# First layer: the softmax division moved behind the value products, and contexts split into high and low parts on GpSimd

## The reference

```
# layer 0: grouped attention, 32 query heads on 8 key/value heads, head size 16
q = x @ Wq + bq;  k = ctx @ Wk + bk;  v = ctx @ Wv + bv
attn = softmax(q k^T / 4 + mask);  out = (attn @ v) @ Wo + bo
x = layernorm(out + x) * gamma + beta
# layers 1 and 2: layernorm, cross attention with 16 heads of 128 and one learnt
# extra key and value (bias_k, bias_v), added to x
# last: x + gelu(layernorm(x) @ w_fc1 + b_fc1) @ w_fc2 + b_fc2
```

## Time and profile before

| | |
|---|---|
| median of three runs | 2411.67 us |
| profiled execution, its time | 2410.44 us |
| its span on the core | 2408.3 us |
| PE busy in the span | 97% |
| layer 0 loop of a half, t0(1) to t0(28) | 107.0 us (half 0), 107.6 us (half 1) |

### The profile page before, as it was taken

How to read it: one execution, slowest core, us unless ns; L and a number is a source line. 1 busy time by engine, 2 the same in 40 slices (tenths; PEclk the granted TensorE clock), 3 DMA queues, 4 the chain that set the end, 5 groups by cost and what they waited for, 6 DMA issues and landing times.

```text
span 2408.3 us, 35904 instructions
## 1 busy us (share of the span) xinstructions
PE 2336.5 (97%) x13616; PEld 1959.0 (81%) x13616; DVE 1210.4 (50%) x2037; ACT 870.4 (36%) x2511; POOL 813.9 (34%) x599
## 2 busy tenths in 40 slices
...
DMA packets 37797, 120.54 MB, mean 50 GB/s; under 512 B 3616, under 2 KB 3872, under 8 KB 37664
## 3 DMA queue, kind: packets, MB, share of 16 engines
...
## 4 chain that ended last, share of the span: by engine, by line
PE 85%; POOL 7%; ACT 3%; DVE 3%; issue 2%; DMA 0%; SPq 0%; POOLq 0%; ACTq 0%; DVEq 0%
PE PS L643 72%; PE PS L871 5%; PE PS L887 5%; PE PS L879 2%; POOL XN L471 1%; POOL HF L471 1%; POOL X L505 1%; ACT AT L1252 1%; POOL W L495 1%; POOL XN L464 1%; POOL P0D L471 1%; ACT PS L1252 1%; POOL W L420 1%; PE PS L743 0%; POOL P0D L464 0%
## 5 line engine op out<-in xcount | busy, mean ns | idle before, releaser
L643 PE MATMUL PS<-AT,W 128*128 128x512 f32 x2496 | 602.8, 391 | 8.7 <-DVE AT L1549 7.8
L643 PEld LDWEIGHTS PS<-AT,W 128*128 128x128 f32 x2496 | 465.3, 188 | 114.0 <-DVE AT L1549 14.8
L1428 DVE TENSOR_TENSOR X<-PS,X 128x512 f32<-128x512 f32 x416 | 286.1, 690 | 360.6 <-PE PS L643 353.5
L542 POOL TENSOR_TENSOR PR<-PR,RC 128x512 f32<-128x512 f32 x128 | 133.4, 1042 | 951.0 <-DVE RC L1636 951.0
L643 PE MATMUL PS<-W,CX 128*128 128x512 f32 x1632 | 403.8, 398 | 7.7 <-DVE Q L1453 4.1
L643 PE MATMUL PS<-CT,W 128*128 128x512 f32 x1584 | 394.2, 398 | 11.0 <-DVE CT L1423 11.0
L643 PE MATMUL PS<-WV,CT 128*128 128x512 f32 (+1 forms) x1920 | 367.1, 349 | 0.0
L643 PEld LDWEIGHTS PS<-W,CX 128*128 128x128 f32 x1632 | 298.0, 188 | 73.4 <-issue 8.3
L643 PEld LDWEIGHTS PS<-WV,CT 128*128 128x128 f32 x1920 | 308.7, 189 | 45.5 <-issue 0.8
L643 PEld LDWEIGHTS PS<-CT,W 128*128 128x128 f32 x1584 | 289.6, 189 | 65.7 <-issue 11.2
L1279 ACT ACTIVATE CX<-PS,VEC 128x512 fp32r<-128x512 f32 x128 | 88.3, 690 | 648.1 <-PE PS L887 648.1
...
## 6 DMA issues: line engine op xcount, KB each, us to landing
...
```

Of the source, the lines that this page charges most:

```text
L542: nc.gpsimd.tensor_tensor(PR[:, :, 0:P], PR[:, :, 0:P], RC[:, 0, 0:BT].unsqueeze(2).to_broadcast([P, BT, P]), ALU.mult).then_inc(norm_done, 1)
L643: ins = nc.tensor.matmul(out, lhs(c, a), rhs(c, b), start=(k == 0), stop=(k == total - 1))
L1428: V_.tensor_tensor(X[:, tile, :], PS[:, bank, :], X[:, tile, :], ALU.add).then_inc(done, 1)
```

## The change

The product with the reciprocals (`norm`) goes. PE transposes the probabilities as they come from the exponentials, and the context of a unit is multiplied with the reciprocals instead, once in four steps. For that the reciprocals of a step are widened from 8 to 128 columns (`widen`, POOL), transposed by PE (`rt0`) into score columns 256 to 511 of banks BS and BS+1, which were spare, and read from there by DVE (`cxnorm0`). ACT evicts the raw context (`cxraw0`); POOL makes its high and low parts (`context`). Three heads are first added in halves on POOL (`half_sums`), and DVE sums 192 columns where it summed 384. `bv` is added with the values. DVE adds a row tile (`row0`) between the mask's add and the maximum, and `rec0(s)` comes in step s behind them, where `rec0(s + 1)` stood ahead. The tables `SPLIT_AT` and `BO_AT` are spread anew (24 pieces and 8 tiles as before; two pieces each in steps 22 and 23), and at the end keys and values of layer 1 change places and banks. The diff, with its indentation reduced and cut to its core:

```diff
-BO_AT = {8: 0, 9: 1, 10: 2, 11: 3, 16: 4, 17: 5, 18: 6, 19: 7}
+BO_AT = {8: 0, 9: 1, 10: 2, 11: 3, 12: 4, 14: 5, 16: 6, 19: 7}
...
+CXF = in_arena("CXF", [P, 3, 2, BTOK], F32, 36864)
...
+HS = BVR[:, 1024:1024 + (KV0 - OWN) * P].rearrange("p (s h t) -> p s h t", s=2, t=P // 2)
+RC0 = BVR[:, 1536:2048].rearrange("p (s n) -> p s n", n=P)
...
-BANKS_FIRST, BANKS_TURN = (BPV, BB, BS, BS + 1), (BA, BB, BS, BS + 1)
-LAST_ROWS = (BS, BS + 1, BA, BPT)
+BANKS_FIRST, BANKS_TURN = (BS, BS + 1, BB, BPT), (BA, BB, BS, BS + 1)
+LAST_ROWS = (BA, BPT, BPV, BC)
...
-    def norm(s):
+    def half_sums(s):
+        pool.wait_ge(exp0, hf * STEPS0 + (s + 1))
+        if s >= 2:
+            pool.wait_ge(rc0, hf * STEPS0 + (s - 1))
+        z = P0[s % BUFS0].rearrange("p (h t) -> p h t", t=P)[:, OWN:KV0, :]
+        nc.gpsimd.tensor_tensor(HS[:, s % 2, :, :], z[:, :, 0:P // 2], z[:, :, P // 2:P], ALU.add).then_inc(half0, 1)
+    def widen(s):
         pool.wait_ge(rc0, hf * STEPS0 + (s + 1))
-        z = P0[s % BUFS0].rearrange("p (h t) -> p h t", t=P)
-        nc.gpsimd.tensor_tensor(z, z, RC[:, s % 2, :].unsqueeze(2).to_broadcast([P, KV0, P]),
-                                ALU.mult).then_inc(norm0, 1)
+        if s >= 4:
+            pool.wait_ge(rt_ps, hf * STEPS0 + (s - 3))
+        copy_hi(RC0[:, s % 4, :].rearrange("p (h d) -> p h d", d=HD0),
+                RC[:, s % 4, :].unsqueeze(2).to_broadcast([P, KV0, HD0])).then_inc(wide0, 1)
+    def context(u):
+        pool.wait_ge(cx0_n, hf * UNITS0 + (u + 1))
+        copy_hi(CX0[:, u % 3, 0, :], CXF[:, u % 3, 1, :]).then_inc(cx0_hi, 1)
+        pool.wait_ge(cx0_hi, hf * UNITS0 + (u + 1))
+        nc.gpsimd.tensor_tensor(CX0[:, u % 3, 1, :], CXF[:, u % 3, 1, :], CX0[:, u % 3, 0, :].bitcast(F32),
+                                ALU.subtract).then_inc(cx0_lo, 1)
...
-    norm(0)
     sub(2)
+    half_sums(0)
     for s in range(STEPS0):
-        if s + 1 < STEPS0:
-            norm(s + 1)
         if s == STEPS0 - 2:
             first_rows()
         if s + 3 < STEPS0:
             sub(s + 3)
+        if s + 1 < STEPS0:
+            half_sums(s + 1)
+        widen(s)
+        if s % 4 == 0 and s:
+            context(s // 4 - 1)
         if s in BO_AT:
             add_bo_tile(BO_AT[s])
...
+    context(UNITS0 - 1)
...
     def t0(s):
-        pe.wait_ge(norm0, s0 + (s + 1))
+        pe.wait_ge(exp0, s0 + (s + 1))
...
-            pe.wait_ge(cx0_lo, u0 + u)
+            pe.wait_ge(cx0_raw, u0 - hf + u)
...
+    def rt0(s):
+        pe.wait_ge(wide0, s0 + (s + 1))
+        pe.wait_ge(z0, s0 + min(s + 5, STEPS0))
+        if s % 4 == 0 and s:
+            pe.wait_ge(cx0_n, u0 + s // 4)
+        nc.tensor.transpose(PS[:, BS + s % 4 // 2, 256 + s % 2 * P:256 + (s % 2 + 1) * P], RC0[:, s % 4, :],
+                            IDENT[:]).then_inc(rt_ps, 1)
...
         if s == 0:
             k0(1)
         else:
+            rt0(s - 1)
             pv0(s - 1)
         if s + 4 < STEPS0:
             s0_(s + 4)
...
         if s == STEPS0 - 4:
             pe.wait_ge(z0, s0 + STEPS0)
-            keys(n1, 0, 0, w1, BS)
+            values(n1, 0, w1, None, (0, 1))
         if s == STEPS0 - 3:
-            values(n1, 0, w1, None, (0, 1))
+            values(n1, 0, w1, None, (2, 3))
         if s == STEPS0 - 2:
-            values(n1, 0, w1, None, (2, 3))
+            pe.wait_ge(xadd, x0 + 3 * BT)
+            keys(n1, 0, 0, w1, BA)
+    rt0(STEPS0 - 1)
     pe.wait_ge(w_ready[3], nq + G0)
+    pe.wait_ge(cx0_lo, u0 + UNITS0 - 1)
     pe.wait_ge(k_ev, n1 * 2 + 1)
     last_rows0(0, 0)
+    pv0(STEPS0 - 1)
     last_rows0(1, 0)
-    pv0(STEPS0 - 1)
     last_rows0(2, 0)
+    pe.wait_ge(v_ev, n1 * 2 + 1)
     last_rows0(3, 0)
     pe.wait_ge(cx0_lo, u0 + UNITS0)
...
         def first_unit():
-            norm_t(norm_index(hf, ly), 0, BANKS_FIRST, range(1))
+            norm_t(norm_index(hf, ly), 0, BANKS_FIRST, range(2))
             pe.wait_ge(k_ev, b0 * 2 + 2)
-            norm_t(norm_index(hf, ly), 0, BANKS_FIRST, range(1, 2))
-            for c in range(2, C):
-                pe.wait_ge(xadd, x_count(hf, b0) - BT + c - 1)
-                norm_t(norm_index(hf, ly), 0, BANKS_FIRST, (c,))
-            pe.wait_ge(v_ev, b0 * 2 + 1)
+            norm_t(norm_index(hf, ly), 0, BANKS_FIRST, range(2, 3))
+            pe.wait_ge(xadd, x_count(hf, b0) - BT + 2)
+            norm_t(norm_index(hf, ly), 0, BANKS_FIRST, range(3, C))
+            pe.wait_ge(v_ev, b0 * 2 + 2)
+            pe.wait_ge(xadd, x_count(hf, b0))
             values(b0 + 1, 1, lv, None, (0, 1))
-            pe.wait_ge(v_ev, b0 * 2 + 2)
             values(b0 + 1, 1, lv, None, (2,))
-            pe.wait_ge(xadd, x_count(hf, b0))
             queries(b0, 0, 0, lq, at_now)
...
-        nc.scalar.activation(VT[:, tb, :], PS[:, BB, :], ACT.Copy).then_inc(vt_ev, 1)
+        nc.scalar.activation(VT[:, tb, :], PS[:, BB, :], ACT.Identity, bias=VEC[:, COL_BV0:COL_BV0 + 1]).then_inc(vt_ev, 1)
...
-    def cxhi0(u):
+    def cxraw0(u):
...
-        nc.scalar.activation(CX0[:, u % 3, 0, :], PS[:, BB, :], ACT.Identity,
-                             bias=VEC[:, COL_BV0:COL_BV0 + 1]).then_inc(cx0_hi, 1)
+        nc.scalar.activation(CXF[:, u % 3, 1, :], PS[:, BB, :], ACT.Copy).then_inc(cx0_raw, 1)
...
+    def rtev0(u):
+        act.wait_ge(rt_ps, s0 + (u * 4 + 4))
+        act.wait_ge(o0_ps, hf * ROWS0 + (u - 1) // 2 * 4)
+        nc.scalar.activation(CXF[:, u % 3, 0, :].rearrange("p (a n) -> p a n", a=2), PS[:, BS:BS + 2, 256:512],
+                             ACT.Copy).then_inc(rt_ev, 1)
...
         if s % 4 == 0 and s:
-            cxhi0(s // 4 - 1)
+            cxraw0(s // 4 - 1)
         if s + 3 < STEPS0:
             e0(s + 3)
         if s == STEPS0 - 4:
-            first_keys(0, BS)
             warm(ACT.Sqrt)
-    cxhi0(UNITS0 - 1)
+        if s == STEPS0 - 2:
+            first_keys(0, BA)
+    rtev0(UNITS0 - 1)
...
+    def soft0(s, row=None):
...
+        if row is not None:
+            row0(row)
...
         dve.wait_ge(exp0, s0 + (s + 1))
-        V_.tensor_reduce(SUM0[:, s % 2, OWN:KV0], P0[s % BUFS0].rearrange("p (h t) -> p h t", t=P)[:, OWN:KV0, :],
-                         AXX, ALU.add).then_inc(sum0, 1)
-        if s >= 2:
-            dve.wait_ge(norm0, s0 + (s - 1))
+        dve.wait_ge(half0, s0 + (s + 1))
+        V_.tensor_reduce(SUM0[:, s % 4, OWN:KV0], HS[:, s % 2, :, :], AXX, ALU.add).then_inc(sum0, 1)
+        if s >= 4:
+            dve.wait_ge(wide0, s0 + (s - 3))
         dve.wait_ge(sum0, s0 + (s + 1))
-        V_.reciprocal(RC[:, s % 2, :], SUM0[:, s % 2, :]).then_inc(rc0, 1)
-    def cxlo0(u):
-        dve.wait_ge(cx0_hi, u0 + (u + 1))
-        V_.scalar_tensor_tensor(CX0[:, u % 3, 1, :], PS[:, BB, :], VEC[:, COL_BV0:COL_BV0 + 1],
-                                CX0[:, u % 3, 0, :].bitcast(F32), ALU.add, ALU.subtract).then_inc(cx0_lo, 1)
+        V_.reciprocal(RC[:, s % 4, :], SUM0[:, s % 4, :]).then_inc(rc0, 1)
+    def cxnorm0(u):
+        cx = CXF[:, u % 3, 1, :].rearrange("p (a n) -> p a n", a=2)
+        if u == UNITS0 - 1:
+            dve.wait_ge(pv0_ps, s0 + STEPS0)
+            dve.wait_ge(rt_ev, hf + 1)
+            ins = V_.tensor_tensor(CXF[:, u % 3, 1, :], PS[:, BB, :], CXF[:, u % 3, 0, :], ALU.mult)
+        else:
+            dve.wait_ge(cx0_raw, u0 - hf + (u + 1))
+            dve.wait_ge(rt_ps, s0 + (4 * u + 4))
+            if u < UNITS0 - 2:
+                dve.wait_ge(s0_ps, s0 + (4 * u + 9))
+            ins = V_.tensor_tensor(cx, PS[:, BS:BS + 2, 256:512], cx, ALU.mult)
+        ins.then_inc(cx0_n, 1)
...
     for s in range(STEPS0):
-        if s + 1 < STEPS0:
-            rec0(s + 1)
-        if s % 4 == 1 and s > 1:
-            cxlo0(s // 4 - 1)
         if s - 2 in Q_AT:
             qlo0(Q_AT[s - 2])
+        row = s - 1 if s - 1 in ROWS_AT else None
         if s + 3 < STEPS0:
-            soft0(s + 3)
+            soft0(s + 3, row)
+        elif row is not None:
+            row0(row)
         if s == 0:
             klo0(1)
-        if s - 1 in ROWS_AT:
-            n, t = ROWS_AT[s - 1]
-            if n < 2:
-                dve.wait_ge(bo_tile, hf * SEQ + (n * BT + t + 1))
-            add0(n, t, BA)
+        rec0(s)
+        if s % 4 == 0 and s:
+            cxnorm0(s // 4 - 1)
...
-    cxlo0(UNITS0 - 1)
+    cxnorm0(UNITS0 - 1)
```

More of the change, by code:

```diff
@@ L47 @@
 SPLIT_AT = {0: (3, (0,)), 1: (3, (1,)), 2: (3, (2,)), 3: (3, (3,)), 4: (0, (0,)), 5: (0, (1,)), 6: (0, (2,)), 7: (0, (3,)),
-            12: (2, (0,)), 13: (2, (1,)), 14: (2, (2,)), 15: (2, (3,)), 20: (1, (0, 1)), 21: (1, (2, 3)),
-            22: (3, (0,)), 23: (3, (1,)), 24: (3, (2, 3)), 25: (0, (0,)), 26: (0, (1,)), 27: (0, (2,)), 28: (0, (3,))}
+            11: (2, (0,)), 13: (2, (1,)), 15: (2, (2,)), 16: (2, (3,)), 17: (1, (0,)), 18: (1, (1,)), 20: (1, (2,)), 21: (1, (3,)),
+            22: (3, (0, 1)), 23: (3, (2, 3)), 25: (0, (0,)), 26: (0, (1,)), 27: (0, (2,)), 28: (0, (3,))}
 PIECES = sum(len(parts) for _, parts in SPLIT_AT.values())
```

(15 more changed lines are left out.)

8 lines of the change are left out of this document (5 added, 3 removed).

## The result

The changed kernel takes 2418.25 us, median of ten runs (2417.62 to 2419.97), where the kernel before takes 2411.65, also of ten (2409.78 to 2413.64): the ratio is 1.0030, with a 95% interval of 1.0022 to 1.0038. It is 6.6 us slower; I had said 8.3 us faster.

A forecast was written before the change was run, and what follows sets the result against it. PE, busy 97% of the span, was taken to bound the kernel, leaving gains only in layer 0's loops: 4.45 us in half 0 and 3.85 in half 1, together 8.3, from 2411.67 to 2403.4 us; range 2395 to 2411.

The forecast's parts named there:

- Half 0: 4.45. Half 1: 3.85. Together 8.3: Gains in us summed over layer 0's loops and their end: 2.0 + 0.85 + 1.0 + 0.6 and 1.4 + 0.85 + 1.0 + 0.6.
- the three rivals: All of PE's waits go, 2396.1 us (chance 0.12); no change, 2410.8 us (0.19); slower, 2427 us (0.07).
- signs of being wrong: Layer 0: `rt0` waits with out0; PE waits for ACT over 2 us per half, t0(8)-t0(22); DVE waits for half sums.
- the rival that I called slower: In full steps of layer 0, PE also waits for the reciprocals' transpose; at 0.5 us each, 2427 us; chance 0.07.
- The other two signs: PE waiting for ACT's evictions over 2 us per half between t0(8) and t0(22); DVE waiting for the half sums.
- Steps 1 to 7: Start of layer 0's loops: ACT sets the pace instead of POOL; 2.0 us gained in half 0, 1.4 in half 1.
- Steps 8 to 21: Middle of layer 0's loops: PE's work 54.3 us plus 1.5, 55.9 in all; 0.85 us gained per half.
- the light pair: Steps 14 and 15 of layer 0: ACT and late reciprocals make them 5.9 us against PE's 4.4, 1.5 more.
- Steps 22 to 27: Late in layer 0's loops: POOL's chain of widenings, pieces and context puts t0(28) at 23.0 us; 1.0 gained per half.
- The end: From t0(28) on: DVE's chain gains 1.1 us, the last context through POOL loses 0.5; net 0.6 gained per half.
- POOL's costs: Layer 0, per step: half sums 0.60 us, widened reciprocals 0.35; a context 1.9 us once in four steps.

The follow-up runs named there:

- e2: The changed kernel with SUM0 allocated behind the arena, so that the arena begins where it did in the kernel before; 2406.84 us, ratio 0.9983.
- e1: The kernel before with RC and SUM0 at the changed kernel's size, so that the arena begins 128 bytes later; 2423.64 us, ratio 1.0053.
- e9: e2 with DVE's row tile behind the maximum, as in the kernel before, not between mask add and maximum; 2404.97 us, ratio 0.9971.
- e8: e2 with DVE's product of a context behind the next mask add, where e2 has it ahead; 2410.46 us.
- e10: e2 without POOL's half sums, DVE summing all 384 columns itself; 2405.6 us, ratio 0.9976.

## Why the prediction was wrong

**The step that failed.** "Half 0: 4.45. Half 1: 3.85. Together 8.3": the sum has terms for layer 0 alone and takes every matmul behind it at its old length. The two enlarged tables were costed at nothing, without a word on what they move. That missing term measured 11.7 us (5.9 and 5.8 in e2's layers against the changed kernel's), larger than the whole forecast and of the other sign; e1 and e2 show it from both sides. None of the three rivals had it.

My signs of being wrong looked at the loops alone. One came up: `rt0` waits in a step with out0, step 25, 1.5 us for POOL's widening in each half, in the changed kernel and in e2 alike (below, half 0 of e2). It is that one of the 12 such steps, so the rival that I called slower did not come about as a loss in all full steps. I had put these waits in steps 22 to 24. The other two signs stayed away: between t0(8) and t0(22) PE waits 0.5 us for ACT's evictions in half 0 of e2, and DVE does not wait for the half sums.

```profile
135.14 0.33 PE L792 MATMUL PS<-IDENT,BVR 128*128 128x128 f32 x1 [1.49 <-POOL BVR L424]
...
137.08 1.19 PE L668 MATMUL PS<-W,CX 128*128 128x512 f32 x4 [0.48 <-POOL CX L492]
```

**The terms for layer 0**, read in e2, against the earlier trace rows:

*Steps 1 to 7* (forecast 2.0 and 1.4): 0.65 by t0(1), as forecast 0.6, and 0.55 behind it, 1.2; and 1.1 in half 1. The waits went from POOL to DVE: the scores' spare columns make `rt0` wait until the mask add of step s+4 has read them. I had named what is queued behind `rt0`, but of its two waits only POOL's.

*Steps 8 to 21* (forecast 55.9, so 0.85 gained): 57.27 and 57.18, 0.5 lost. Two terms were mis-sized. PE's work is 55.24 us by its busy time, where I had 54.3: my 52.6 for the kernel before lay 0.6 under its 53.22, and the 14 new transposes added 2.0, 0.14 each (0.11 where nothing waits; I had 0.12). That is 0.9 of the 1.4 us in half 0. The other 0.5 is idle time, 2.0 us where I had 1.5 for the light pair (54.3 + 1.5 is 55.8, not 55.9) and nothing for step 8, nor for q, whose waits fell from 2.2 to 0.7 us and did not go. DVE waits more than before, when it waited 0.8 us for ACT's context copy and not at all for out0:

```profile
DVE X L1471 <- PE PS L668: 2.8, 7, 0.8
DVE CXF L1540 <- ACT CXF L1222: 1.7, 3, 0.7
```

How much each of these is worth stays open: e9, with the row tile elsewhere, recovers 0.1 to 0.25 us of it, e8 none.

*Steps 22 to 27* (forecast 23.0, gained 1.0): 22.66 and 22.68, gained 1.3 and 1.4. POOL's chain sets the pace, as named: e10 takes 0.60 us a step out of it and gets 1.2 back.

*The end* (forecast 0.6): 0.3. The last 12 matmuls wait for POOL's context, as said, 0.5 to 0.6 us.

*POOL's costs.* The groups that answer to the earlier trace rows, 30 to 160 us of the changed kernel:

```profile
L477 POOL TENSOR_TENSOR BVR<-XN 128x192 f32<-128x192 f32 x16 | 11.0, 688 | 0.0
...
L424 POOL TENSOR_SCALAR BVR<-RC 128x128 f32<-128x128 f32 x31 | 9.3, 300 | 1.1 <-DVE RC L1527 1.1
L492 POOL TENSOR_TENSOR CX<-CXF,CX 128x512 fp32r<-128x512 f32 x7 | 9.0, 1284 | 0.6
```

The reciprocals took 0.30 (I took 0.35), a context 0.62 + 1.28 (1.9). The half sums' 688 is a mean over two early ones of 1.05 and 1.58 us; single ones in e2's loop take 0.59 to 0.61 (0.60). The rows' slope, 2.2 ns a column taken down from the 734 ns for 256, gave the whole instruction. POOL's share of steps 8 to 21 fell from 99 to 88%. So POOL's durations were right; what was wrong lay outside them.

In all the loops gave 4.5 us (2.3 and 2.2), with e2's median as well, not 8.3. 11.7 - 4.5 is 7.2 and the measured loss 6.6; the difference is within what stretches of lower clock move between runs.
